# A graph network layer on one core: one load of four tile numbers per gather group, histograms with contiguous weights, and a finer order of blocks at the end

## The reference, cut to what matters

```python
# 1. graph convolution over 200000 edges (src, dst), dst sorted
deg  = segment_sum(1, dst) + 1
norm = rsqrt(deg)[src] * rsqrt(deg)[dst]
out  = segment_sum(xw[src] * norm, dst)          # xw = MLP(x) @ w_gcn.T
# 2. linear attention over all nodes, 8 heads, added with x to out, layer norm
# 3. attention over a second graph (131072 edges and self loops), which yields
#    scores of 4 experts per node; top 2 kept; then for each expert e
out += g[..., e] * (gelu(x @ W1[e] + b1[e]) @ W2[e] + b2[e])
```

## Time and profile before

| | us |
|---|---|
| median of three runs | 6648.84 |
| lowest, highest of them | 6631.96, 6654.02 |
| the profiled execution's own time | 6612.06 |
| its span, first to last instruction | 6610.4 |
| PE busy (matmuls) | 4430.7 |
| POOL busy | 2901.8 |
| DVE busy | 2593.8 |
| ACT busy | 758.7 |

### The profile page before, as it was taken

The page is one execution under the profiler, slowest core; times in us unless marked ns, Lnnn a source line. Parts: engine busy times, 40 slices in busy tenths (PEclk is TensorE's granted clock), DMA queues, the critical chain, the costliest instruction groups (busy, mean ns, idle before and its releaser), DMA issues. The chain is left out here.

```text
span 6610.4 us, 50389 instructions
## 1 busy us (share of the span) xinstructions
PE 4430.7 (67%) x14755; PEld 3046.5 (46%) x14755; DVE 2593.8 (39%) x5223; ACT 758.7 (11%) x1439; POOL 2901.8 (44%) x2919
## 2 busy tenths in 40 slices
PE   6998777888788887777754325764775485451264
PEld 6887544444455555666644113442443253230143
DVE  5555565565554445555554000220221121113244
ACT  1112311212000000000011001110111011010111
POOL 0000466666655556777710772334434523552300
PEclk8667989888776777777755557876876697675687
DMA  2112433333444443333465211221221121211265
GB/s 68 50 50 51 138 114 113 109 116 112 114 129 124 128 116 93 92 90 91 88 132 148 37 9 41 50 50 25 50 50 26 35 64 27 45 31 39 54 174 140
DMA packets 241863, 531.52 MB, mean 80 GB/s; under 512 B 73332, under 2 KB 147415, under 8 KB 234822
## 3 DMA queue, kind: packets, MB, share of 16 engines
q1 hardware_dynamic: 121909, 293.42, 16.4%
q0 software_dynamic: 119696, 235.05, 15.1%
HBM read 377.97 MB, written 150.28 MB: 80 GB/s over the span
## 5 line engine op out<-in xcount | busy, mean ns | idle before, releaser
L923 POOL DMA_INDIRECT g_rows<-table,gcn_srcT x1664 | 1707.0, 1026 | 915.9 <-issue 460.9
L1768 POOL DMA_INDIRECT n_rows<-gtab,so_own x1122 | 1081.7, 964 | 1246.6 <-DVEq L1885 905.5
L993 PE MATMUL g_ps<-g_rows,g_hot 128*125 128x256 f32 x3328 | 1082.3, 463 | 262.8 <-DVE g_hot L1259 172.0
L1716 PE MATMUL p_py<-f_w,f_hh 128*125 128x256 f32 x2688 | 723.0, 407 | 791.8 <-issue 791.6
L1271 DVE TENSOR_TENSOR acc<-acc,g_ps 125x256 f32 x1664 | 700.6, 421 | 1004.1 <-PE g_ps L993 339.1
L1716 PEld LDWEIGHTS p_py<-f_w,f_hh 128*125 128x125 f32 x2688 | 539.2, 201 | 994.9 <-issue 932.3
L993 PEld LDWEIGHTS g_ps<-g_rows,g_hot 128*125 128x125 f32 x3328 | 702.8, 229 | 514.2 <-issue 210.4
L1909 DVE TENSOR_TENSOR p_ob<-p_py,p_xb 125x512 f32<-125x512 f32 x168 | 114.6, 691 | 1971.0 <-remote 1031.1
L1710 PE MATMUL p_ph<-f_xfT,f_w 128*128 128x500 f32 x1344 | 652.9, 628 | 258.6 <-issue 190.3
L1710 PEld LDWEIGHTS p_ph<-f_xfT,f_w 128*128 128x128 f32 x1344 | 270.2, 201 | 604.6 <-issue 601.3
L1938 ACT ACTIVATE f_hh<-p_ph,f_b 128x500 f32<-128x500 f32 x336 | 224.3, 677 | 1955.7 <-remote 1143.1
(11 more groups left out here) (322 smaller groups left out, 4183.4 us busy)
## 6 DMA issues: line engine op xcount, KB each, us to landing
o_d<-p_ob SPq DMA_DIRECT2D x21, 1920.0 KB
z_ob<-o_d SPq DMA_DIRECT2D x21, 1920.0 KB
g_rows<-table,gcn_srcT POOLq DMA_INDIRECT x1664
n_rows<-gtab,so_own POOLq DMA_INDIRECT x1122
gout<-n_o SPq DMA_DIRECT2D x11, 1224.0 KB
xnT_d<-a_xnT SPq DMA_DIRECT2D x25, 500.0 KB, 3.0
m_area<-xnT_d SPq DMA_DIRECT2D x25, 500.0 KB
qT_d<-m_area SPq DMA_DIRECT2D x25, 500.0 KB
```

The lines of the kernel that those rows point to most:

```text
L923: pool.indirect_dma_start(out=rows[:, g % RING, j], out_offset=None, in_=K.table, in_offset=bass.IndirectOffsetOnAxis(ap=K.gcn_srcT[:, 4 * ...
L993: mm = pe.matmul(ps[q, p % 4, b], hot[:, g % 3, 2 * j + b], rows[:, g % RING, 2 * j + b], start=True, stop=True, skip_group_check=True)
L1716: mm = pe.matmul(py[0:TN, e % 2, j // 2, (j % 2) * D:(j % 2 + 1) * D], self.hh[:, e % 2, c, j * TN:(j + 1) * TN], self.w2[:, e, c], start= ...
L1768: pool.indirect_dma_start(out=rows[:, c % 3, j], out_offset=None, in_=K.gtab, in_offset=bass.IndirectOffsetOnAxis(ap=K.gat_src[:, c * W + ...
```

## The change

1. In the gather a group's four tile numbers are fetched with one load instruction that fills four registers, without the range checks; `hot` is built two groups ahead instead of one, with a fourth buffer.
2. In both histograms `ot` becomes the weights and is laid out with the tile numbers innermost, so that each weight load reads 100 contiguous values; `on` (125 columns, still with a step of 16) is streamed. The result is then by tile first, and is copied and transposed once at the end.
3. In the finale the list goes by single experts of late blocks: two ready blocks, then after each of the 16 (late block, expert) pairs one or two ready ones.

```diff
-    for out, ids, width, sem in ((on, K.gcn_node, TN, node_s), (ot, K.gcn_tile, NT, tile_s)):
-        dve.tensor_tensor(out[0:c, r % 2], number[0:c, 0:width],
-                          ids[0:c, r * HB:(r + 1) * HB].unsqueeze(1).to_broadcast([c, width, HB]),
-                          ALU.is_equal).then_inc(sem, 1)
+    dve.tensor_tensor(on[0:c, r % 2], number[0:c], K.gcn_node[0:c, cols].unsqueeze(1).to_broadcast([c, TN, HB]),
+                      ALU.is_equal).then_inc(node_s, 1)
+    wide = [c, HB, NT]
+    dve.tensor_tensor(ot[0:c, r % 2], K.iota_h[0:c, 0:NT].unsqueeze(1).to_broadcast(wide),
+                      K.gcn_tile[0:c, cols].unsqueeze(2).to_broadcast(wide), ALU.is_equal).then_inc(tile_s, 1)
...
-    mm = pe.matmul(pdeg[q], on[0:c, r % 2, :, b], ot[0:c, r % 2, :, b], start=r == 0 and b == 0,
+    mm = pe.matmul(pdeg[0:NT, 0, q], ot[0:c, r % 2, b], on[0:c, r % 2, :, b], start=r == 0 and b == 0,
...
+    pe.transpose(pdeg[q, 1, 0:NT], by_tile[0:NT], K.ident[0:NT, 0:NT]).then_inc(both_s, 1)
...
     def build(g):
-        if g >= 3:
-            dve.wait_ge(mm_s, 2 * (g - 2))
+        if g >= 4:
+            dve.wait_ge(mm_s, 2 * (g - 3))
...
-    def add(p):
-        tiles = [dve.value_load(K.gcn_tiles[0:1, 2 * p + b:2 * p + b + 1], min_val=0, max_val=NT - 1)
-                 for b in range(2)]
+    def tiles_of(g):
+        _, four = nc.values_load_multi_w_load_instructions(
+            K.gcn_tiles[0:1, 4 * g:4 * g + 4], [mybir.EngineType.DVE], min_val=0, max_val=NT - 1,
+            skip_runtime_bounds_check_because="...")
+        return four
+    def add(p, tiles):
         dve.wait_ge(mm_s, p + 1)
...
-    if p % 2 == 0 and p // 2 + 1 < S_GCN // 4:
-        build(p // 2 + 1)
-    add(p)
+    if p % 2 == 0:
+        tiles = tiles_of(p // 2)
+        if p // 2 + 2 < S_GCN // 4:
+            build(p // 2 + 2)
+    add(p, tiles[p % 2 * 2:p % 2 * 2 + 2])
...
+    parts = len(late) * NE
+    ahead = [HEAD + (EARLY - HEAD) * (n + 1) // parts for n in range(parts)]      # HEAD = 2
+    order = [("ready", i) for i in range(HEAD if parts else EARLY)]
+    for n in range(parts):
+        order.append(("late", n))
+        order += [("ready", i) for i in range(ahead[n - 1] if n else HEAD, ahead[n])]
```

More of the change, by code:

```diff
@@ L59 @@
 EARLY = 21
+HEAD = 2
 def blocks(eng, body):
@@ L992, in gathered @@
                     for b in range(2):
-                        mm = pe.matmul(ps[q, p % 4, b], hot[:, g % 3, 2 * j + b], rows[:, g % RING, 2 * j + b],
+                        mm = pe.matmul(ps[q, p % 4, b], hot[:, g % 4, 2 * j + b], rows[:, g % RING, 2 * j + b],
                                        start=True, stop=True, skip_group_check=True)
@@ L1082, in degrees @@
                     for b in range(b0, b0 + 4):
-                        mm = pe.matmul(pa[q, 0:NT], on[:, r % 2, :, b], ot[:, r % 2, :, b], start=r == 0 and b == 0,
+                        mm = pe.matmul(pa[0:NT, q], ot[:, r % 2, b], on[:, r % 2, :, b], start=r == 0 and b == 0,
                                        stop=r == half - 1 and b == HB - 1)
@@ L2048, in finale @@
 def finale(nc, K, A):
-    late = list(range(EARLY, NB))
-    order = []
-    for i, k in enumerate(late):
-        order += [k] + list(range(EARLY * i // len(late), EARLY * (i + 1) // len(late)))
-    ready = [k for k in order if k < EARLY]
+    late, ready = list(range(EARLY, NB)), list(range(EARLY))
+    parts = len(late) * NE
[4 more added lines that the diff above has]
+        order += [("ready", i) for i in range(ahead[n - 1] if n else HEAD, ahead[n])]
     RING = 3
@@ L2114, in _ @@
                     sp.dma_start(row[:, n], a.rearrange("(a o) -> a o", a=1).to_broadcast([P, GW])).then_inc(row_s, 16)
-                load_late(0)
+                if late:
+                    load_late(0)
                 for i in range(RING):
                     load_early(i)
-                load_late(1)
-                for k in order:
-                    if k in late:
-                        i = late.index(k)
-                        store_late(i)
-                        if i + 2 < len(late):
-                            load_late(i + 2)
-                    else:
-                        i = ready.index(k)
+                if late:
+                    load_late(1)
+                for kind, i in order:
+                    if kind == "ready":
                         store_early(i)
@@ L2182, in _ @@
                 act.activation(sc[q], sc[q], ACT.Exp).then_inc(ex, 1)
-                gelu(0, 0)
-                gelu(0, 1)
+                for n in range(min(2, parts)):
+                    gelu(0, n)
                 act.wait_ge(gated, 1)
-                for k in order:
-                    if k in late:
-                        i = late.index(k)
-                        for e in range(2 if i == 0 else 0, NE):
-                            gelu(i, e)
-                    else:
-                        first_part(ready.index(k))
+                for kind, i in order:
+                    if kind == "ready":
+                        first_part(i)
+                    elif 2 <= i + 1 < parts:
+                        gelu((i + 1) // NE, (i + 1) % NE)
             @block.vector
@@ L2279, in weigh_early @@
                                                      ).then_inc(sum_s, 1)
-                for k in order:
-                    if k in late:
-                        weigh_late(late.index(k))
+                for kind, i in order:
+                    if kind == "ready":
+                        weigh_early(i)
                     else:
-                        weigh_early(ready.index(k))
+                        weigh_late(i // NE, i % NE)
 def program(nc, A):
```

98 lines of the change are left out of this document (59 added, 39 removed).

## The result

The changed kernel takes 6429.42 us, the median of four runs (6419.1 to 6434.06), against 6650.91 of the kernel before, also in four runs: a ratio of 0.968, 95% interval 0.966 to 0.970, 221 us less. The forecast was 6300 with 6190 to 6440, and 6220 to 6380 for its likeliest case, so the time lies inside the whole range and outside that of the case that I held likeliest. The profiled execution took 6419.1 us (6612.06 before), 193 us less.

What follows compares the result with a forecast made beforehand. PE was taken to bound the first half, engines waiting on each other the gather, PE and DMA in turn the finale. Terms -50 + 3 - 185 - 115 = -347 gave 6302 from the median 6649, said as 6300; range 6190 to 6440.

Steps and rivals of the forecast that it cites:

- New pace 0.205: Histograms, PE: a turned matmul takes 0.205 us instead of 0.236, 50 us less over 1600 in the first half.
- the bound of 0.236: Histograms, PE: if a streamed column costs the load's 1.89 ns, a matmul stays at 0.236 us and nothing is saved.
- Slower: Rival, TensorE's clock: low in the gather, up to 922 us more; conversely 34 us less in the first half; chance 0.03.
- The rival of an unslowed stream: First histogram: the step costs nothing, a matmul needs at most 0.105 us, DVE sets the pace, -130, 6222 us; chance 0.07.
- Histogram, DVE: Histograms: `ot` goes from 984 ns to 1.81 us on DVE, hidden by its wait for PE or free time; 0 taken.
- DVE's 204 less a quarter ... leaves 150: Gather: of 204 us of DVE idle before the adds, 150 become gain, a quarter lost where PE or ACT is late.
- 35 for `hot`: Gather: the fourth `hot` buffer gains 35 us, a fifth of PE's 172 us of waits for it.
- the loads were covered anyway: Rival, gather: DVE's idle before the adds only changes its name to waits for PE; gather -50, 6437 us; chance 0.13.
- the bound of 455 us: Gather: the most that could be gained, all the time POOL's fetches are held back by PE or others.
- Finale: Finale: PE and DMA work together instead of in turn, ending at about 6493 instead of 6607, 115 us less.
- The lists do wait for each other: Rival, finale: ready blocks not landed hold back ACT's next gelu, gain 50 instead of 115, 6367 us; chance 0.06.
- the 14.6 us an expert: Finale: time allowed for each of 16 experts, 234 us, against 13.6 of PE and 14.2 of DMA, for mutual waits.

Runs made afterwards that it cites:

- gather_alone: The kernel before with only the gather's part (one load of four tile numbers a group, `hot` two groups ahead): ratio 0.986 to the kernel before.
- both_contiguous: The changed kernel with `on` of the first histogram also laid out without a step, so neither operand has one: ratio 0.967 to the kernel before.
- finale_alone: The kernel before with only the finale's finer order: ratio 0.983 to the kernel before.

## Why the prediction was right or wrong

**Histogram, PE (-50; -27).** The step that failed is "New pace 0.205", with the reading of the earlier trace rows under it: 100 streamed columns in 0.16 us, scaled to 0.205 for 125. Measured: 0.227, 1.8 ns a column, near the bound of 0.236 that the prediction kept, and worth 6 us of the stage. The other 21 us came from the projection at a higher clock, a case that the prediction names under *Slower*, with 34 us, and left out of its sum. So that half of the 50 appeared was luck. The 0.16 is the distance of a load's recorded start from a matmul's, not of two matmuls, and was too little to rest a slope on. The Trainium skill (Advanced Engine Details and Errata, Memory Cachelines) has a penalty for each element on a new line; with both operands contiguous the spacing is 0.106 and 0.058, so the trace agrees that it is the step that costs, at 1.82 ns a column streamed. On the weights it is 1.86 ns a column, if load and stream lie beside each other as the prediction took it; no run has a step on the weights alone. The prediction's sentence that by this rule the part would save nothing came nearer than its 50. The rival of an unslowed stream is out.

**Histogram, DVE (1.81 us, hidden).** Measured 1.818, and hidden in both: DVE's wait for PE shrank from 207 to 106 us. In the second histogram the cover was not where the prediction put it. It counted DVE's free time; the price came on POOL, 51 us of longer fetches, and was hidden only because POOL had 60 us to spare.

**Gather (-185; -65 in the profile, -96 alone).** The failed step is "DVE's 204 less a quarter ... leaves 150", and with it "35 for `hot`". The waits did vanish nearly as counted (205 us of `issue`, 134 of those for `hot`). But only in the second attention pass did that shorten the stage: 63 us there, 10 in the first pass, nothing in the last stretch. By the distances of the adds, 22 of the 63 us lie in its short slots 1 to 5, where DVE's queue could have set the pace; 41 lie in slots 6, 7 and 0, with PE's products, where the clock has its share. Elsewhere DVE waited for PE's product instead, as the rival "the loads were covered anyway" said, to which I gave 0.13. Its 6437 is nearest to the result, in part by luck: its histogram gives 23 us too much and its gather 15 too little. The 35 for `hot` were nothing. The one load of four registers is not dear: it takes 0.34 us in DVE's queue, and the wait before `hot` is 10 us. Behind this stands a thing that none of the cases had: in long runs of fetches PE's work is drawn out with no wait that the profile can name, so POOL's "own work" and PE's chain are not independent, and the bound of 455 us, all that POOL is held, is not a bound of what lies between them. Shown is that the late products and 616 us of the gather go with three quarters of the fetches. That part 1 would have given more without them is argued, not shown.

**Finale (-115; -116).** The mechanism held: PE and DMA are busy together, DMA at 204 to 219 GB/s against the 245 of the earlier trace rows. Of the terms, the start took 40 us instead of 46, PE's work from there to its last down matmul 230 instead of 234, and the end 25 instead of 14, because the last ready block's load lands late; that the sum is right to 1 us is in part these offsets. The lists do wait for each other, as the rival says, but the 14.6 us an expert had room for that.

**The rest.** Ends of the histograms +1.6 for the first. The expert stage and what lies around it grew by 12 us, with no edit there; gather_alone and both_contiguous have 2850 and 2846 us there, finale_alone 2847, the kernel before 2831, so it is spread. TensorE's clock moved little over the span, from 0.737 to 0.748, but not so by stages, as shown. Sum of the profile's parts: -27 + 2 - 65 + 12 - 116 = -194, of 193 measured. The time lies 11 us inside the upper end of the range, which reached so far in order to take in the covered loads.

## What to carry to other kernels

Before a sum of waits is turned into a gain, ask stretch by stretch who would be waited for next: of 339 us of waits that vanished here, 65 to 96 came back as time. When a stage gets shorter, compare the granted clock and the matmuls that the change does not touch before crediting the edit: 21 of the first histogram's 27 us were the projection's. A stage that the profile shows idle on every engine, with "issue" or "remote" as releaser, is worth an experiment of its own before one tunes beside it: here 11 fetches at a time instead of 102 gave 631 us where the gather's part gave 96. And a matmul with a step between the elements of one operand was as slow as with steps in both (0.227 and 0.233 us); to be rid of the cost both had to be contiguous, and the engine that builds them then becomes the limit.

## What the runs showed of the hardware

- One kernel, two kinds of chip: 6626 and 5462 us for the kernel before; one chip of the faster kind was seen. On the slower kind PE issues about one instruction to each of POOL's indirect DMAs once a burst has gone on for 20 to 25 us, at 1.2 GHz (clock 0.50); on the faster kind 696 matmuls in 200 us beside as many fetches, at 2.4 GHz (1.00). What differs between the chips, or whether it is the chip or something else of those runs, is open.
- In the gather on the slower kind, 65 of 147 products reached a waiting DVE more than 1.5 us after their end in PE's record (0.15 us is usual), nearly all in runs of fetches of over 15 us; on the faster kind none did in a run of 979 us. A gap in PE's record beside such products is not idle time.
- A matmul with a 32-byte step on its streamed operand takes 0.227 us for 125 columns, whatever the clock (5th to 95th percentile 0.226 to 0.228 at a mean granted clock of 0.68); without a step 0.106 us at 1.2 GHz and 0.058 at 2.4. The 0.106 is near what the Trainium skill (TensorE: Matmul & The Clock Gate, Back-to-back issue gap) gives for the lower level, N/1.2 ns, 104 ns.
- An indirect DMA of 128 rows takes POOL 946 ns, and 1503 on average beside a 1.82 us DVE comparison of two SBUF operands.
- The granted clock shows in matmuls that an edit leaves alone: the projection's 200 matmuls took 120 us at a mean of 0.65 and 99 at 0.68.
